# Attention block with split-precision matmuls on one core: an earlier spread of values, a later low part of Wo, and heads ahead of exponentials

## The reference

```python
xn = layernorm(x, g_in)
q = (xn @ Wq).reshape(b, n, H, DH).transpose(0, 2, 1, 3) * scale
kv = xn @ Wkv
k, v = (kv[..., :DH], kv[..., DH:])
k, v = null key / value ahead of k, v
sim = einsum('bhid,bjd->bhij', q, k) + bias        # bias: null column, then attn_bias
sim = where(causal or masked, -max, sim)
out = einsum('bhij,bjd->bhid', softmax(sim), v)
out = layernorm(out.transpose(0, 2, 1, 3).reshape(b, n, INNER) @ Wo, g_out)
return x + out
```

## Time and profile before

| | |
|---|---|
| median of the runs | 1016.31 us |
| the profiled execution | 1017.48 us, its span on the core 1015.7 us |
| mean granted clock of PE | 0.995 of full speed |
| PE busy | 989.0 us (97%) |
| POOL busy | 834.8 us (82%) |
| DVE busy | 767.9 us (76%) |
| ACT busy | 658.6 us (65%) |

### The profile page before, as it was taken

The page is one execution under the profiler, slowest core; times in us unless marked ns, Lnnn a source line. Parts: engine busy times, 40 slices in busy tenths (PEclk is TensorE's granted clock), DMA queues, the critical chain, the costliest instruction groups (busy, mean ns, idle before and its releaser), DMA issues.

```text
span 1015.7 us, 43757 instructions
## 1 busy us (share of the span) xinstructions
PE 989.0 (97%) x14250; PEld 869.1 (86%) x14250; DVE 767.9 (76%) x3553; ACT 658.6 (65%) x2622; POOL 834.8 (82%) x1503
## 2 busy tenths in 40 slices
PE   7889999999999999999999999999999999999987
PEld 5879888888888888888888888888888888888875
DVE  5976787777887777787777887777787777786664
ACT  5846676665676665676665676666676666675563
POOL 4877888888888888888888888888888888888786
PEclk9998999999999999999999999999999999999999
DMA  8422223223232332323323232232323223222112
GB/s 240 118 79 73 86 72 87 82 68 98 64 107 73 80 87 60 105 69 87 79 70 96 68 106 72 76 90 55 109 70 86 78 71 96 68 70 67 37 44 63
DMA packets 93774, 84.04 MB, mean 83 GB/s; under 512 B 25328, under 2 KB 67824, under 8 KB 93552
## 3 DMA queue, kind: packets, MB, share of 16 engines
q1 hardware_dynamic: 92496, 81.05, 29.9%
q10 hardware_dynamic: 1056, 0.04, 0.1%
HBM read 40.12 MB, written 16.78 MB: 56 GB/s over the span
## 4 chain that ended last, share of the span: by engine, by line
PE 89%; POOL 4%; SPq 3%; issue 2%; DVE 1%; DMA 1%; ACT 1%; POOLq 0%; DVEq 0%; ACTq 0%
PE ps_proj L569 39%; PE ps_pv L546 22%; PE ps_pv L553 11%; PE ps_s L507 10%; PE ps_pv L532 8%; SPq L369 1%; POOL bias_b L1222 1%; POOL w_nrm L1231 1%; DMA q_sb<-in_fside_16xSxS_dram 0%; SPq L344 0%; SPq L379 0%; SPq L338 0%; POOL bias_c L1320 0%; POOL y_nrm L1271 0%; POOL y_out L1275 0%
## 5 line engine op out<-in xcount | busy, mean ns | idle before, releaser
L1031 ACT ACTIVATE exp_bot<-logit_bot,neg_max 128x129 f32<-128x129 f32 x512 | 201.4, 398 | 211.0 <-DVE neg_max L693 208.2
L1222 POOL TENSOR_TENSOR bias_b<-bias_c,mask_add 128x256 f32<-128x256 f32 (+1 forms) x512 | 297.9, 612 | 26.8 <-DVE neg_max L693 26.4
L569 PE MATMUL ps_proj<-xt_hi,wq_hi 128*128 128x256 f32 x1024 | 299.0, 292 | 6.0 <-ACT v_raw L1083 3.7
L569 PE MATMUL ps_proj<-xt_hi,wq_lo 128*128 128x256 f32 x1024 | 285.0, 278 | 0.0
L569 PE MATMUL ps_proj<-xt_lo,wq_hi 128*128 128x256 f32 x1024 | 284.6, 278 | 0.0
L693 DVE CUSTOM_DVE_ANT_0 logit_bot<-ps_s,bias_b 128x128 f32<-128x128 f32 x512 | 128.5, 289 | 139.7 <-PE ps_s L507 123.1
L569 PEld LDWEIGHTS ps_proj<-xt_hi,wq_hi 128*128 128x128 f32 x1024 | 193.4, 189 | 21.2 <-issue 10.5
L1231 POOL TENSOR_TENSOR w_nrm<-exp_bot,w_inv 128x256 f32<-128x256 f32 x256 | 157.9, 617 | 63.0 <-DVE w_inv L702 61.6
L546 PE MATMUL ps_pv<-wo_hi,o_hi 128*128 128x512 f32 x488 | 194.1, 398 | 1.5 <-DVE o_lo L715 1.4
L569 PEld LDWEIGHTS ps_proj<-xt_hi,wq_lo 128*128 128x128 f32 x1024 | 194.0, 189 | 0.7 <-issue 0.5
L569 PEld LDWEIGHTS ps_proj<-xt_lo,wq_hi 128*128 128x128 f32 x1024 | 193.6, 189 | 0.0
(11 more groups left out here) (114 smaller groups left out, 1747.3 us busy)
## 6 DMA issues: line engine op xcount, KB each, us to landing
x_in<-in_x_dram SPq DMA_DIRECT2D x32, 512.0 KB, 4.1
x_split<-xn SPq DMA_DIRECT2D x480, 32.0 KB, 1.9
v_rep<-v_raw SPq DMA_DIRECT2D x256, 32.0 KB, 1.9
x_res<-in_x_dram SPq DMA_DIRECT2D x128, 64.0 KB, 1.9
x_res<-in_x_dram SPq DMA_DIRECT2D x64, 128.0 KB, 2.6
out_dram<-y_out SPq DMA_DIRECT2D x128, 64.0 KB, 1.7
out_dram<-y_out SPq DMA_DIRECT2D x64, 128.0 KB, 2.3
w_raw<-in_L_cond_Wq_dram SPq DMA_DIRECT2D x4, 512.0 KB, 7.6
```

The costliest lines, as they stand in the source:

```text
L569: mm = pe.matmul(ps[:, 0:TOK], w[:, k, cols], xt[:, slot, k], start=(j == 0), stop=(j == len(todo) - 1))
L1031: ins = nc.scalar.activation(out_[:, s, j], in_[:, s, j], ACT.Exp, bias=neg_max[:, s, k:k + 1], scale=-1.0, accum_out=w_sum[:, s, k:k + 1])
L1222: ins = nc.gpsimd.tensor_tensor(out_, bias, key_mask, ALU.add)
```

## The change

Three edits. On SP, in the first pair, `spread_v(1)` comes before `next_mask`, `split_x(3)` and `next_x(1)` rather than behind them. On POOL, the last low part of Wo also waits until DVE has made its three (`wo_lo_made` at 3). On ACT, in all steps of `body`, the heads come ahead of both exponentials.

```diff
                 if first:
                     split_x(BY_PE)
                     next_x(0)
+                    spread_v(2 * p + 1)
                     next_mask()
                     split_x(2 * p + 3)
                     next_x(1)
-                    spread_v(2 * p + 1)
...
-                    if t < CP and t % CG != STEP_HEADS:
-                        exponentials(n, t, 1)
                     for batch, back in due("heads", p, t, first, last):
                         for g in range(4):
                             heads_hi(batch, g)
-                    if t < CP and t % CG == STEP_HEADS:
+                    if t < CP:
                         exponentials(n, t, 1)
-                    if t < CP:
                         exponentials(n, t, 0)
...
                 pool.wait_ge(wo_hi_made, WP)
+                pool.wait_ge(wo_lo_made, WP - 1)
                 nc.gpsimd.tensor_tensor(wo_piece(wo_lo, WP - 1), ...).then_inc(last_wo_lo_made, 1)
```

## The result

| | before | changed |
|---|---|---|
| median of four runs | 1017.31 us (1016.21 to 1018.83) | 1010.59 us (1007.37 to 1011.57) |
| profiled execution, its span | 1017.48 us, 1015.7 us | 1007.37 us, 1005.6 us |
| mean granted clock, profiled execution | 0.995 | 0.999 |
| mean granted clock, the other three | | 0.996, 0.996, 0.997 |
| DVE busy | 767.9 us | 797.9 us |

The ratio is 0.9928 with an interval of [0.9905, 0.9951]: faster by 6.7 us in the medians, where 10.9 was forecast, and the median lies 0.1 us above the top of the range with rivals (1002.8 to 1010.5) and 3.1 above the forecast's own (1003.5 to 1007.5). The forecast of 1005.5 started from a median before of 1016.31 us; over four runs this is 1017.31, so 1.0 us of the distance lies in the start value and 4.2 in the gain. The two profiled executions differ by 10.1 us.

A forecast was written before the change was run, and what follows sets the result against it. PE, busy 97%, bounds the kernel, apart from a start-up hole and small losses at steps 6 and 14. 1017.48 - 6.1 - 0 - 4.8 = 1006.6, as median 1005.5 us; range 1003.5 to 1007.5, with the first three rivals 1002.8 to 1010.5.

The forecast's parts named there:

- The hole for `v_raw`: Start-up, group 2: PE stands 3.67 us before q projections, then runs at half clock; 6.6 us together.
- The term of 6.1 us: Start-up: the earlier spread on SP brings the scores of step 14 from 83.95 to 77.85.
- Wo's low part: Start-up: POOL's part behind DVE's lets PE project by Wo 1.4 us earlier, swallowed at `split_x(3)`; net 0.
- Heads ahead of exponentials: ACT, steps 6 and 14: heads start 1.64 instead of 1.89 us after the values; 4.8 us back.
- All 4.9 us: Steps 6 and 14: summed excess over 0.36 us from PE's last filler matmul to the second by Wo.
- the price: ACT stands for PE's values, `exp_top` ends 0.5 us later, delaying `inverse`; costed at 0, uncovered 15 us.
- The fourth rival (slower): Loop: ACT standing for PE holds up exponentials in 30 steps, PE waits for weights; 1025 us, chance 0.03.
- rival 1: Start-up: the clock falls again behind PE's remaining 2.2 us pause, costing 2.9 us; 1008.4 us, chance 0.12.
- the 2.9 us: Start-up: cost of half clock during group 2's four q projections, 8.45 us instead of 5.5.
- rivals 2 and 3: Steps 6 and 14 do not recover, chance 0.08; the start-up gives only 1.4 us, chance 0.07; each 1010.2 us.

The follow-up runs named there:

- A: The kernel before with only SP's spread of values issued earlier in the first pair: 1011.00 us, ratio 0.996.
- C: The kernel before with only ACT's heads put ahead of both exponentials in all steps: 1011.94 us, ratio 0.9955.
- A and C: The kernel before with SP's earlier spread and ACT's heads first, without POOL's wait: 1005.98 us; on a third chip 1006.40 us.
- B: The kernel before with only POOL's last low part of Wo waiting for DVE's: 1014.74 us, ratio 0.9989.
- the longer pause: A and C plus an extra 1.2 us transpose on DVE ahead of `turned(3)` in the first pair: 1007.98 us, ratio 0.9922.
- `turned(3)` last: A and C, with DVE's `turned(3)` behind statistics, values and inverse of its step in the first pair: 1007.55 us; third chip 1005.02 us.
- all three edits with `turned(3)` last: The changed kernel, with DVE's `turned(3)` behind statistics, values and inverse of its step in the first pair: 1007.23 us, ratio 0.9917.

## Why the prediction was right, and where it was off

**The hole for `v_raw`: right.** A alone removes it, with C or without. In the profiled execution the scores of step 14 came at 77.63 where 77.85 was forecast, `turned(3)` at 69.52 where it said 69.5, `project_out(0)` at 48.07 where it said 48.4. Two errors cancel in this: the spread took 0.8 us more than 5.00 and `split_x(3)` 1.1 less than 11.80. With a slower spread (A alone) the part is worth 4.9. The term of 6.1 us was priced as if the one row of SP held at the new place: the eight spreads took 5.00 or 5.01 us in all four traces without A, and 5.60 to 6.94 in the ten with A, in each of which at least one issue was longer than 0.6.

**Wo's low part: right in place and price.** 1.22 us, PE earlier by 1.85 at step 12 (1.75 forecast), most of it swallowed. Alone it gave 0.7 us, with an interval that reaches zero, beside A and C nothing that can be told. The forecast of 0 stands.

**Heads ahead of exponentials: the mechanism right, the size too large.** All 4.9 us at steps 6 and 14 went away, and 3.6 to 3.8 arrived in the loop. Over all traces the loop, from step 14 of the first pair to the last pair, took 892.9 to 894.4 us in the three with the old order of ACT and 887.0 to 891.2 in the ten with C: 4.0 us apart on the mean, with a scatter as large as the gain. In the place of the rest came longer "issue" pauses, which the sum had no term for; that C brings them is not shown: A alone had 4.0 us of them, and A with C in one trace 2.9. Of the price the prediction saw the wait of `inverse` for ACT (now 22.2 us in all) and its cover. It did not see `xt_lo`, 32 us of DVE. DVE's pauses for PE covered both. The fourth rival (slower) is refuted: PE never came to wait for `wt` (0.6 us in the whole run).

**The clock: the step that failed.** The forecast put 0.12 on rival 1, a clock that falls again, and took the difference between profiled execution and median over from the kernel before. The profiled execution had the full clock. A mean of 0.998 or 0.999 is what the end of the span alone makes: every trace has half clock there for 1.4 to 4.5 us, behind PE's last matmul. Of 16 runs of the changed kernel on three occasions 9 had a mean clock of 0.997 or less, with a median of 1010.7 us, and 7 had more, with 1007.4: 3.3 us apart, near the 2.9 of that rival, and 3.0 to 3.6 us apart on each occasion. Without B, A had one such run of 34 (A; A and C; these with the longer pause or with `turned(3)` last), and all three edits with `turned(3)` last none of 6. So among the kernels without the hole for `v_raw` the low clock goes with two things together, a pause before q 3 and B. Why is open. B brings PE to the pause earlier, but A and C with DVE first by chance had a longer pause (2.36 us) at full clock, if only in one trace. No execution of the changed kernel with a low clock was profiled, so where it was low is not seen.

Of 39 runs of the kernel before, beside the experiments, 5 had a mean of 0.998 or 0.999 and lay only 0.6 us under the median of their group, so the 2.9 us that the prediction read as the clock's price from one trace is not borne out by these. The Trainium skill, "TensorE: Matmul & The Clock Gate", Part 1, has the clock throttled unless activity releases it; the traces agree for four pauses of 2.42 to 3.67 us (0.50 with or behind each, for 3.4 to 7 us), and not for seven of 0.56 to 2.36 us, all at the full clock.

**The median.** From the profiled 10.1 to the measured 6.7 us: the low clock in three of the four runs explains about 3 us in each of them. The rest is scatter: runs of A alone at one clock span 4 us. That the median came within 0.1 us of the range is in part luck: its upper edge was set by rivals 2 and 3, in which the loop or the start-up gives little, and neither took place. Over the occasions the changed kernel was 6.7, 5.1 and 8.8 us under the kernel before beside it, always faster and always by less than 10.9.

## What to carry to other kernels

Look for what stands in an engine's program between a producer on PE and the copy that PE needs back. Most of it is paid on PE, with its waits: two exponentials cost 0.16 us a step, and the same two with a wait for another engine 0.75. A start-up hole that a DMA queue's order makes is fixed by that order, but ask what is late next and whether a pause is left in front of matmuls: with the last pause taken out (`turned(3)` last) none of 18 runs had the low clock. And a profiled execution at the full clock is not the median when the clock falls only in some runs; the list of clocks shows it.

## What was not expected of the hardware

- Two instructions on DVE and POOL that start within 0.11 us of each other: with starts within 0.01 us, DVE takes 3.46 and POOL 2.38 us (seven traces); with DVE first by 0.11 us, 1.24 and 3.38 (two). The one that comes second stands for the other's length or what is left of it (2.2 and 1.0 us more than 1.22 and 2.4). The Trainium skill, "SBUF — State Buffer", section "SBUF: two separate sides", has this as first come first served, and the traces agree.
- Moving ACT's order alone made `xt_lo` on DVE 57% longer (935 to 1469 ns): it now runs at the same time as POOL's work. The mean is 935 or 936 ns in the four traces without C, and 1463 to 1471 in all ten with C. Between 200 and 330 us its median is 1778 ns against 922 before. That it is POOL that holds it up was read from the timeline and not tested apart.
- Single DMA issues on SP of up to 2.1 us among others of 0.6: the eight of one spread took 5.00 to 6.94 us.
- The mean clock was 0.997 or less in 9 of 16 runs of one and the same program, and a pause of 2.42 us was followed by half clock where one of 2.36 us in another kernel was not.
